# AdaLN block with global and windowed attention: the running maxima lead by 12 key tiles instead of 16, and the divisions and the small products move within each head

## The reference

```python
q = (x @ Wq).reshape(b, l, 16, 64); k, v = ... 4 heads each, repeated 4 times   # rotary applied to q and k
attn = einsum('bhqd,bhkd->bhqk', q, k) / 8 + slopes[h] * (pos_k - pos_q)
out = softmax(attn) @ v;  x = x + ga * (out.reshape(b, l, 1024) @ Wo)
```

## Time and profile before

| | us |
|---|---|
| median of 3 runs (lowest, highest) | 1161.92 (1161.27, 1162.92) |
| the profiled execution's own time | 1160.41 |
| its span | 1158.6 |
| PE, DVE, POOL, ACT busy | 1078.5, 900.7, 721.6, 637.3 |
| first and last start of L825 (the maxima) | 108.3, 681.7 |
| first and last start of the head loop's score products, L916 | 127.6, 711.9 |

### The profile page before, as it was taken

The page is one execution under the profiler, slowest core; times in us unless marked ns, Lnnn a source line. Parts: engine busy times, 40 slices in busy tenths (PEclk is TensorE's granted clock), DMA queues, the critical chain, the costliest instruction groups (busy, mean ns, idle before and its releaser), DMA issues. The chain is left out here.

```text
span 1158.6 us, 23134 instructions
## 1 busy us (share of the span) xinstructions
PE 1078.5 (93%) x8352; PEld 662.9 (57%) x8352; DVE 900.7 (78%) x1584; ACT 637.3 (55%) x1000; POOL 721.6 (62%) x526
## 2 busy tenths in 40 slices
PE   6784799999999999999999999779999898999988
PEld 4552445555554555455455546637777695777678
DVE  6995768777877788777887765669988589888867
ACT  3442365666566566666656654046666455666554
POOL 3662266667666666766666675699986337666526
PEclk9996799999999999999999999979999999999999
DMA  8899421524315143252333200201111100111111
GB/s 257 280 276 343 91 65 38 119 51 105 69 44 120 38 91 75 65 114 44 79 79 74 47 12 20 92 9 31 33 37 37 26 2 19 32 32 33 33 26 36
DMA packets 83457, 89.03 MB, mean 77 GB/s; under 512 B 32740, under 2 KB 66064, under 8 KB 83344
## 3 DMA queue, kind: packets, MB, share of 16 engines
q1 hardware_dynamic: 83344, 87.55, 29.9%
HBM read 53.57 MB, written 24.25 MB: 67 GB/s over the span
## 5 line engine op out<-in xcount | busy, mean ns | idle before, releaser
L825 DVE CUSTOM_DVE_ANT_0 junk<-psum,alibi 128x1024 bf16<-128x1024 f32 x256 | 312.6, 1221 | 135.2 <-PE psum L892 126.3
L797 ACT ACTIVATE E<-psum,keybias_sb 128x1024 f32<-128x1024 f32 x256 | 275.0, 1113 | 178.9 <-PE psum L916 165.6
L734 POOL TENSOR_TENSOR xpos_sb<-xpos_sb,E 128x1024 f32<-128x1024 f32 x96 | 231.3, 2410 | 127.8 <-ACT E L797 123.3
L928 PE MATMUL psum<-E,V 128*64 128x512 f32 x1024 | 247.9, 605 | 0.0
L892 PE MATMUL psum<-KH,QH 64*128 64x512 f32 x512 | 121.2, 469 | 15.8 <-DVE M L825 8.2
L928 PEld LDWEIGHTS psum<-E,V 128*64 128x64 f32 x1024 | 62.1, 136 | 117.7 <-issue 111.3
L738 POOL TENSOR_TENSOR xpos_sb<-xpos_sb 128x1024 f32<-128x1024 f32 x32 | 76.0, 2376 | 68.9 <-DVE xpos_sb L835 68.9
L892 PEld LDWEIGHTS psum<-KH,QH 64*128 64x128 f32 x512 | 49.7, 190 | 109.8 <-DVE M L825 93.3
L916 PE MATMUL psum<-QH,KH 64*128 64x512 f32 x512 | 102.4, 396 | 0.7 <-DVE M L825 0.7
L916 PE MATMUL psum<-QL,KH 64*128 64x512 f32 x512 | 101.5, 392 | 0.0
L916 PE MATMUL psum<-QH,KL 64*128 64x512 f32 x512 | 101.4, 392 | 0.0
(11 more groups left out here) (145 smaller groups left out, 2088.9 us busy)
## 6 DMA issues: line engine op xcount, KB each, us to landing
QH<-qa_scratch SPq DMA_DIRECT2D x64, 256.0 KB, 4.7
qa_scratch<-tH SPq DMA_DIRECT2D x8, 1024.0 KB, 5.6
qa_scratch<-tL SPq DMA_DIRECT2D x8, 1024.0 KB, 7.9
QL<-qa_scratch SPq DMA_DIRECT2D x64, 128.0 KB, 4.8
XF<-inverse_scratch SPq DMA_DIRECT2D x32, 256.0 KB, 3.5
vp_att<-v_att SPq DMA_DIRECT2D x64, 128.0 KB, 2.3
KH<-k_scratch SPq DMA_DIRECT2D x16, 256.0 KB, 4.0
KL<-k_scratch SPq DMA_DIRECT2D x16, 256.0 KB, 5.3
```

What stands on the lines that cost most here:

```text
L734: pool.tensor_tensor(sum_p[:, s, :], first, E[:, k % 4, :], ALU.add)\
L797: act.activation(E[:, k % 4, :], scores(k % 2), ACT.Exp, bias=kb).then_inc(exp_done, 1)
L825: dve.tensor_tensor_reduce(junk[:, :], banks(max_bank(i, k), 2), alibi[:, s, :], -1.0, BIG, ALU.add, ALU.min, M[:, s, k:k + 1]).then_inc(m ...
L928: last = pe.matmul(banks(6 + i % 2)[HD * ch:HD * ch + HD, :], V[:, g, k, :], E[:, k % 4, ch * 512:(ch + 1) * 512], start=(k == 0), stop=(k ...
```

## The change

The lead becomes 12 tiles (`LEAD = TB + TB // 2`): 12 maxima stand ahead of head 0, and in head i, slot k, the one of tile 8i + k + 12 counted through all heads is made. `small_products(i)` goes from behind the pv of pair 2 to pair 4, behind its first max and ahead of its pv. ACT takes its results ahead of exponential 6, the maxima first. `invert` goes from slot 6 of the next head to slot 3 of the one after; SP's `spread_inverse` is cut into `spread_denominators(i-1)` and `widen_inverse(i-2)`. The four divisions of a pair, from slots 1 to 4 of an odd head, go to slots 2 and 6 of the even head i that starts two heads after the pair ended its own, and slots 1 and 2 of the odd head behind it. The last pair but one is divided after the loop.

```diff
+            LEAD = TB + TB // 2
+            def max_ahead(i, k):
+                return divmod(TB * i + k + LEAD, TB)
             def max_bank(i, k):
-                return 4 if i >= 2 else (4, 0, 2)[(TB * i + k) % 3]
+                return 4 if TB * i + k >= LEAD else (4, 0, 2)[(TB * i + k) % 3]
...
                         if i > 0:
-                            spread_inverse(i - 1, (i - 1) % 2)
+                            spread_denominators(i - 1, (i - 1) % 2)
+                        if i > 1:
+                            widen_inverse(i - 2, i % 2)
...
-                    spread_inverse(HEADS - 1, (HEADS - 1) % 2)
+                    widen_inverse(HEADS - 2, HEADS % 2)
+                    spread_denominators(HEADS - 1, (HEADS - 1) % 2)
+                    widen_inverse(HEADS - 1, (HEADS - 1) % 2)
...
-                            if k == 4 and i > 0:
-                                take_denominators(i - 1)
-                            if k == 4 and i + 1 < HEADS:
-                                take_m(i + 1, (i + 1) % 2)
+                            if k == 6 and i + 1 < HEADS:
+                                take_m(i + 1, (i + 1) % 2)
+                            if k == 6 and i > 0:
+                                take_denominators(i - 1)
...
-                            if i + 2 < HEADS:
-                                max_step(i + 2, i % 2, k)
-                            if 1 <= k <= QUARTERS and i % 2 == 1 and i > 1:
-                                divide((i - 3) // 2, k - 1)
-                            if k == 6 and i > 0:
-                                invert(i - 1, (i - 1) % 2)
+                            if max_ahead(i, k)[0] < HEADS:
+                                max_step(*max_ahead(i, k))
+                            if i >= 4 and k in ((2, 6), (1, 2))[i % 2]:
+                                divide((i - 4) // 2, 2 * (i % 2) + ((2, 6), (1, 2))[i % 2].index(k))
+                            if k == 3 and i > 1:
+                                invert(i - 2, i % 2)
...
+                    invert(HEADS - 2, HEADS % 2)
+                    for n in range(QUARTERS):
+                        divide(HEADS // 2 - 2, n)
                     invert(HEADS - 1, (HEADS - 1) % 2)
...
                             qk_step(i, k + 1)
-                            if i + 2 < HEADS:
-                                max_step(i + 2, k)
+                            if max_ahead(i, k)[0] < HEADS:
+                                max_step(*max_ahead(i, k))
+                            if k == 4:
+                                small_products(i)
                             if k > 0:
                                 pv_step(i, k - 1)
                             elif i > 0:
                                 pv_step(i - 1, TB - 1)
                             pv_step(i, k)
-                            if k == 2:
-                                small_products(i)
```

More of the change, by code:

```diff
@@ L684, in load_m, with spread_denominators @@
                                          mrow[TB // 2 * ch:TB // 2 * (ch + 1), s, :].bitcast(F32)).then_inc(ld_m[s], 16)
-                    def spread_inverse(i, s):
+                    def spread_denominators(i, s):
                         need(sp, den_taken, i + 1)
@@ L692, in spread_inverse, with widen_inverse @@
                                          den_sb[32 * c:32 * c + 1, :].rearrange("o (p e) -> o p e", e=TB)).then_inc(den_in, 16)
+                    def widen_inverse(i, s):
                         need(sp, inv_done, i + 1)
@@ L817, in _, with max_step @@
                 def _(dve):
-                    def max_step(i, s, k):
+                    def max_step(i, k):
+                        s = i % 2
                         need(dve, max_mm, TB * i + k + 1)
@@ L854, in head @@
                                 sum_step(i - 1, (i - 1) % 2, 1)
-                            if i + 2 < HEADS:
-                                max_step(i + 2, i % 2, k)
-                            if 1 <= k <= QUARTERS and i % 2 == 1 and i > 1:
-                                divide((i - 3) // 2, k - 1)
-                            if k == 6 and i > 0:
-                                invert(i - 1, (i - 1) % 2)
+                            if max_ahead(i, k)[0] < HEADS:
[4 more added lines that the diff above has]
+                                invert(i - 2, i % 2)
                             if k == 5:
                                 sum_step(i, i % 2, 0)
-                    for i in range(2):
-                        for k in range(TB):
-                            max_step(i, i, k)
+                    for n in range(LEAD):
+                        max_step(*divmod(n, TB))
                     need_landed(dve, 1)
@@ L886, in max_step @@
                             need(pe, mrow_done, 1 if i >= 2 else 0)
-                        need(pe, max_done, TB * i + k - (2 if i < 2 else 0))
+                        need(pe, max_done, TB * i + k - (2 if TB * i + k < LEAD else 0))
                         for ch in range(2):
@@ L907, in qk_step @@
                             pe.wait_ge(qm_filled, 3)
-                            pe.wait_ge(max_done, 2 * TB - 2 + k)
+                            pe.wait_ge(max_done, LEAD - 1 + k)
                         keys = slice(k * P, (k + 1) * P)
@@ L959, in head @@
                             pv_step(i, k)
-                            if k == 2:
-                                small_products(i)
[L962 to L969, removed]
+                            if max_ahead(i, k + 1)[0] < HEADS:
+                                max_step(*max_ahead(i, k + 1))
+                    for n in range(LEAD):
+                        max_step(*divmod(n, TB))
+                        if n == TB + 2:
+                            turn_m(0, 0)
                     for i in range(HEADS):
```

## The result

The kernel after runs in 1190.72 us (median of 5, 1188.62 to 1192.34) against 1162.06 of the kernel before (5 runs, 1161.27 to 1163.04): ratio 1.0246, 95% interval 1.0234 to 1.0259. Its profiled execution took 1188.62 us, with a span of 1186.8, 28.2 us more than before. The forecast was 1188, with 1183 to 1191 as its own range; the measured median is 2.7 us above the former and at the upper end of the latter.

The account below looks back on a forecast made before the run. PE's own list was taken to set the loop's pace; -4.1 + 1.0 + 14.1 + 19.5 - 4.5 + 0.5 = +26.5 us gave 1188 us. Its own range was 1183 to 1191 (chance 0.66), eight in ten 1172 to 1194.

Parts of the forecast that it names:

- The start: Ahead of head 0: waiting for the 11th maximum instead of the 14th starts it earlier, -4.1 us.
- The maxima moved into the loop: Head 30, slots 0 to 3: four maxima added to PE's work, +1.0 us.
- Even heads: Slot 2: division waits for POOL's addition, PE's max of slot 4 comes late; 1.07 us per head, +14.1 together.
- The race: Even heads, slot 2: POOL's addition starts 0.08 us ahead of DVE's division, which waits for all of it.
- Odd heads: Divisions of slots 1 and 2 wait for POOL, stalling PE's max of slot 4 by 1.5 us; 13 heads, +19.5.
- the 4.5 that went: Odd heads 3 to 29: the old stall of 0.32 us in each of 14 heads disappears, -4.5 us.
- The slot 6 division: Even heads: it waits for POOL's addition; DVE runs 0.4 us late in the odd head that follows.
- Behind the loop: Head 31's denominators queue behind a broadcast waiting for pair 14's four divisions: +0.5 us, bounds 0 and +2.
- B: Rival, chance 0.08: divisions don't meet POOL or idle DVE time absorbs their wait; all heads at 18.27, 1155 us.
- A: Rival, chance 0.14: DVE gets in first in slot 2 of even heads, which lose nothing; 14.1 less, 1174 us.
- C: Rival, chance 0.12: row of maxima late in odd heads, or the start gains less; up to +6, 1194 us.
- the zero put down for SP's queue: Odd heads: row of maxima, queued behind broadcast and query loads, lands hidden; cost 0, up to +0.5 x 13.

Follow-up runs that it names:

- Run 5: Kernel after, with PE's denominators (0.57 us) back behind the pv of pair 2, the turn of M staying at pair 4: 1175.30 us.
- run 7: Kernel after, with POOL's addition of tile 2 in even heads waiting for DVE's division of slot 2: 1176.49 us.
- run 10: Kernel after, both divisions in slot 3, row of maxima first in SP's list, last denominators ahead of head 30's widening: 1156.51 us.
- run 1: Kernel after, with the divisions of the first 14 pairs replaced by one-column reciprocals: 1154.07 us.
- run 3: Kernel after, with a pair's four divisions bunched in slots 1 to 4 of the odd head: 1211.83 us.
- run 2: Kernel after, with both divisions of a head in slot 3: 1157.49 us.
- run 4: Kernel after, with a tiny memset on POOL ahead of its addition of tile 2 in even heads: 1192.00 us.

## Why the prediction was right

**The start** was forecast at -4.1, measured -4.45, of which 0.3 is the earlier start of the stage. The row of maxima was in time.

**The maxima moved into the loop**: head 30 is 1.24 us longer (17.56 against 16.32), as forecast at 1.0 + 0.2.

**Even heads**: 12 of the 13 from 4 to 28 take 19.44 to 19.51, 1.19 above the floor of 18.28 where 1.07 was forecast, and head 12 takes 18.30. So 12 x 1.19 + 0.2 = 14.5 against 14.1. The race, forecast with POOL 0.08 us ahead, went so in all but one head, by 0.07 to 0.10 us, and the one that went the other way was there to be read in the trace before. Run 5 shows the cover lost, and run 7 that the meeting of division and addition costs what was forecast.

**Odd heads**: 19.88, 1.60 above the floor, where 1.5 was forecast; 13 x 1.60 = 20.8 against 19.5, less the 4.5 that went. I named the max of slot 4 as the only place, and said that stretched heads in other slots would mean a wrong replay. In that the text was wrong: the maximum of slot 2, released at +8.2, has its result only at +9.5, so PE already stands at the max of slot 3, +8.4 by its own work. The period didn't suffer, because DVE's chain sets the end of both waits and I had counted it up to slot 4.

**The slot 6 division** takes 1.46 us and delays DVE 0.4 in the odd head, as forecast; its only price is that push.

**Behind the loop**: from the first output projection (742.46) to the first one behind the last pair's divisions (758.67) 16.2 us, before 15.7: +0.5, as forecast, and by the way forecast: the broadcast waits for the four divisions, and the denominators go out behind it, 5.5 us behind the first output projection where it was 4.9.

```profile
745.21 2.08 DVE L863 TENSOR_TENSOR OT<-OT,XF 128x256 f32<-128x256 f32 x4 [1.52 <-DMA XF<-inverse_scratch]
...
747.36 0.48 SPq L707 DMA_DIRECT2D XF<-inverse_scratch  x1
747.93 2.44 SPq L697 DMA_DIRECT2D den<-XF  x4
```

Turning this order round doesn't help, as run 10 showed.

**The loop as a whole** lasts from 123.13 to 742.46, 619.3 us, against 587.3: +32.0 where the terms give 30.1. The missing 1.9 are 1.3 in the odd heads, 0.4 in the even ones and 0.3 in head 0 (19.46 against 19.19). The last is no price of the change that could be told from chance: run 7 has the same code there and takes 18.94. The granted clock, 0.50 at the head's start, rises to 1.00 at about +5.4 us in the kernel after, at +3.1 in the one before and at +3.0 in run 7. The sum of the profiled executions is +28.2 against +26.5 forecast.

**Rivals.** B had the right price (1155 against 1154.07 in run 1) and the wrong condition. A happened in head 12 alone; run 7 brings its price about in all even heads. C was priced at +6 and didn't occur in the kernel after, but I had taken 1.8 us for the DMA of QM with no load ahead of it. Behind four query loads the row was in 3.2 to 4.0 us behind its second DMA's start in run 3. Such loads stand ahead of it in the kernel after as well, and the row had 4.6 to 4.9 us. By run 3's times, an estimate, the zero put down for SP's queue held by some 0.6 us, and not by the 2.6 that I had reckoned.

## What to carry to other kernels

Place a DVE operation with both inputs in SBUF against GpSimd's timeline too, not only against its own engine's list: find the stretch in which GpSimd waits, and put it there, in pairs if need be. From the kernel after to run 2 that was worth 33 us of 1190. Short work of the bounding engine is free only if it stands in front of a wait; moving 0.57 us of it back in front of the wait made every head that waits 0.56 to 0.58 us shorter (run 5). When a DMA's issue is made to wait for a compute step, read what is queued behind it on the same issuing engine, and put what the next head needs first ahead of it.

## What the runs showed of the hardware

Where a division and a POOL addition met, the one that started first took its own time and the other took longer, and the margin is fine. POOL 0.07 us ahead: the division takes 2.60 (run 4); 0.10 ahead: 2.56. DVE 0.20 ahead: 0.42 for the division, and POOL's addition 2.48 instead of 2.38 (head 12). Behind the start of head 31 of the kernel after, both orders stand in one POOL operation, L751:

```profile
727.28 2.93 DVE L863 TENSOR_TENSOR OT<-OT,XF 128x256 f32<-128x256 f32 x2
727.43 2.49 POOL L751 TENSOR_TENSOR xpos_sb<-xpos_sb 128x1024 f32<-128x1024 f32 x1 [1.16 <-DVE xpos_sb L849]
```

The first of the two divisions starts 0.15 us ahead of POOL and takes 0.41 us; the second starts during POOL's operation and ends 0.29 behind its end.

The clock fell in waits that I took for short. Run 3, head 8, behind PE's wait of 2.73 us for QM; the columns are those of the earlier trace rows:

```profile
278.80:285.50 6.70, 6.68 (x26) 3.60 (x26) 1.23 (x2) 2.75 (x3) 3.74 (x2) 0.53 0.16 40
285.50:300.00 14.50, 14.50 (x97) 7.36 (x97) 8.56 (x14) 8.59 (x11) 7.45 (x4) 1.00 0.72 145
```

A granted clock of 0.53 over 6.7 us is mostly the lower level, 1.2 GHz; the head's first two tiles took 7.35 us instead of 4.38. Of the 12 such waits, 7 (1.84 to 2.73 us long) were followed by a slow stretch that cost 1.4 to 3.0 us, and 5 (2.12 to 2.60 us) by none, so the length of the wait alone doesn't decide it; what does isn't shown. From head 1 on, the longest wait of PE's matmuls in the head loop of any other run, 1.3 us in run 2, was followed by none.
